# First layer of a two-layer cross-attention kernel: weighted sum issued behind the scores, three transposed groups finished in their own slot

## The chip, the cores and the metric

The kernel runs on one core of one Trainium2 chip. The time is the device time of one execution in microseconds (us). Three runs of the kernel before took 1789.04, 1791.48 and 1791.99, median 1791.48. A core has five engines with a queue of instructions each: TensorE (PE), VectorE (DVE), ScalarE (ACT), GpSimd (POOL) and SyncE (SP, which here only issues DMAs). They meet only in semaphores.

## What is computed

The input x is 8 batches of 56 rows by 256; the context is 8 batches of 1500 rows by 256. The first layer, the only one the change touches, cut to what matters:

```python
a = _layer_norm(audio_kv, ln_gamma, ln_beta)          # context, 8 x 1500 x 256
Q, K, V = hidden_states @ Wq.T, a @ Wk.T, a @ Wv.T    # 16 heads of 16 columns
scores = einsum('bhtd,bhsd->bhts', Q, K) * scale + mask
attn = softmax(scores, axis=-1)
out = einsum('bhts,bhsd->bhtd', attn, V) @ Wo.T
x = hidden_states + tanh(gate) * out
```

Two cross-attentions with 16 heads of 128 columns and an MLP follow. All matrix products are made of high and low parts: a value is split into a part that TensorE's fast format holds (high) and the rest (low), and three products high·high, high·low, low·high are summed.

## The kernel before

**Slots.** The first layer is 64 slots: 8 batches (`b`) of 8 head pairs (`t`, 0 to 7), `g = 8b + t`. A slot has 112 rows (two heads of 56 queries) and 1500 context columns. Each engine has a function `slot(b, t, n, kind)` which says what it issues in a slot, and `whole_batches` calls it for all slots: batches 0 to 5 are of kind "full", 6 of kind "keys", 7 of kind "plain"; batches 1 to 4 run in a hardware loop. The order within `slot` is written out by hand, and there is no scheduler.

**The path of one slot g.**
- TensorE makes the scores: 3 matmuls of 500 columns into PSUM banks 0 to 2 (`scores`, L841). They wait until the exponential of slot g−1 has read the banks.
- VectorE takes the negated row maximum over all three banks (`row_max`, L1742, written to `neg0`).
- ScalarE makes the exponential with that bias into `prob0` (`softmax`, L1299), with the row sums beside it.
- TensorE turns the 12 chunks of 128 columns of `prob0` in three groups of 4 (`transposes`, L853). Group 0 goes to PSUM bank 3, group 1 to bank 4, group 2 to bank 3 again. Groups 0 and 1 wait for the low parts of the slot before, group 2 for the low part of group 0 of its own slot.
- ScalarE copies a turned group as high part into `pt0` (`high_probs`, L1247, tile pt), and VectorE subtracts it for the low part (`low_probs`, L1667, tile pt).
- TensorE makes the weighted sum: 12 matmuls on `pt0` and the values `v3`, into bank 7 (`weighted`, L870). It waits for all six parts of its slot.
- ScalarE copies the second half of it to `ost` (`output`, L1305), and VectorE adds the first half (`collapse`, L1763, tile o_c).

**Beside it, for the batches to come.** In slots 0 to 5 of kinds "full" and "keys" TensorE makes one sixth of the next batch's keys (`keys`, 6 matmuls of 500 columns into bank 5, L770 to L772), ScalarE copies it to `kst` (L1247), GpSimd splits it into `khl` (L604, L579), and SyncE stacks the parts into `k3` (L393 to L396, 5 DMAs for a head pair). In slots 0 to 3, 6 and 7 TensorE makes one sixth of the values (`values`, 12 matmuls of 256 columns into bank 6), which ScalarE copies at the head of its next slot and VectorE splits there (tile v). For the batch after the next, kind "full" only, VectorE takes statistics of the raw context in slots 0, 1 and 2 (`load_stats`, L1674 and L1680, 4 chunks each), GpSimd makes the factors (`variance`, L583 and L585), TensorE turns them (`turn_stats`, L780), ScalarE sends them to memory and back as one long row for all partitions (`spread_stats`), GpSimd scales the context by it (`scale`, L590) and splits it with ScalarE (`ct_low`, `ct_high`). In slot 4 TensorE spreads the reciprocals of the batch before over the partitions (`spread`, L877).

**How a slot is staged before the change.** In slot g TensorE issues: scores of g+1, group 2 of g−1, keys, weighted sum of g−1, groups 0 and 1 of g, values. ScalarE: high part of group 2 of g−1, copy of the values, copy of the keys, exponential of g+1, copy of the weighted sum of g−1, high parts of groups 0 and 1 of g. VectorE: maximum of g+1, low part of group 2 of g−1, low part of the values, statistics (slots 1 and 2), collapse of g−1, low parts of groups 0 and 1 of g, statistics (slot 0).

**The start.** Before the slots the same engines make the queries, the centred weights (`w0`), the statistics and the split of the contexts of batches 0 and 1, the keys of batch 0 in six groups (`K_FIRST`) and its values. GpSimd's queue there is: factors of batch 0, low parts of the weights, scale of the last third of context 0 (L674), factors of batch 1, low part of that third, three key groups, two scales of batch 1. VectorE's `load_stats(1, k)` stands between the centred weights and the splits of the queries (L1707).

## Time and profile before

| what | value |
|---|---|
| median of 3 runs | 1791.48 us |
| profiled execution | 1799.13 us, span 1797.3 us |
| mean granted TensorE clock | 0.973 |
| TensorE busy | 1672.9 us (93%) |
| VectorE busy | 1203.6 us (67%) |
| ScalarE busy | 1041.9 us (58%) |
| GpSimd busy | 902.7 us (50%) |
| from 0 to 460 us: TensorE busy | 376.49 us |
| from 460 us on: TensorE busy | 1296.36 of 1337.30 us |

The span runs from the first to the last instruction of the profiled execution; its own time is 1.8 us longer. Busy time counts instructions at work. The first 460 us are the first layer. The granted clock is 1.00 for 2.4 GHz and 0.5 for 1.2 GHz; a stretch between has had both.

### The profile page before, as it was taken

The page shows a single profiled execution, that of the slowest core. Times are in us where ns is not written, and L with a number is a line of the kernel's source. Part 1 is how long each engine was busy: PE and PEld are TensorE (multiplying, and loading weights), DVE is VectorE, ACT ScalarE, POOL GpSimd, SP SyncE. Part 2 cuts the span into 40 slices and gives each one's busy share as a digit, 9 for nine tenths or more (in the row PEclk, how much of TensorE's full clock was granted, in tenths as well). Part 3 has the DMA queues.
Part 4 walks back from the last instruction along what each step waited for, and adds up shares of the span by engine and source line. Part 5 has one row for each costly group of instructions (what it writes and reads, how often), then busy time and mean ns, then how long its engine had stood idle before and what let it go on. Part 6 is the DMA issues. An engine that isn't in the chain of part 4 may idle for free.

```text
span 1797.3 us, 36860 instructions
## 1 busy us (share of the span) xinstructions
PE 1672.9 (93%) x12520; PEld 1576.3 (88%) x12520; DVE 1203.6 (67%) x2340; ACT 1041.9 (58%) x2023; POOL 902.7 (50%) x655
## 2 busy tenths in 40 slices
PE   4788988997899999999999999999999999999997
PEld 3677877786789999999999987889999999999986
DVE  5577777777356766766766766466676677677673
ACT  2467766676264655656656555545665656556563
POOL 4456665542144545536535547453653554455483
PEclk8899999999699999999999999899999999999998
DMA  7967666746221111111211114221121121120031
GB/s 211 234 161 183 180 173 177 179 115 167 73 81 62 54 50 37 64 41 36 70 35 36 70 32 131 62 85 37 36 70 36 35 70 36 36 70 1 2 91 40
DMA packets 109995, 150.81 MB, mean 84 GB/s; under 512 B 25540, under 2 KB 95684, under 8 KB 109828
## 3 DMA queue, kind: packets, MB, share of 16 engines
q1 hardware_dynamic: 108484, 142.45, 28.4%
q10 hardware_dynamic: 1344, 6.19, 1.0%
q8 instruction: 98, 1.61, 0.4%
q14 instruction: 69, 0.57, 0.1%
HBM read 108.32 MB, written 3.42 MB: 62 GB/s over the span
## 4 chain that ended last, share of the span: by engine, by line
PE 67%; DVE 10%; ACT 3%; issue 2%; SPq 1%; POOL 1%; DMA 1%; ACTq 0%; DVEq 0%; POOLq 0%
PE ps L770 12%; PE ps L772 11%; PE ps L771 11%; PE ps L1025 7%; PE ps L1029 7%; PE ps L1027 7%; PE ps L960 2%; DVE ar L1866 2%; PE ps L1005 2%; PE ps L992 1%; DVE neg L1742 1%; PE ps L853 1%; PE ps L870 1%; DVE ar L1911 1%; ACT prob L1299 1%
## 5 line engine op out<-in xcount | busy, mean ns | idle before, releaser
L722 POOL TENSOR_TENSOR rr<-ar,rr 125x512 fp32r<-125x512 f32 x336 | 455.3, 1387 | 406.6 <-ACT rr L1483 398.7
L1025 PE MATMUL ps<-cx,rr 125*128 125x258 f32 x1344 | 396.6, 295 | 0.0
L1029 PE MATMUL ps<-cx,rr 125*128 125x258 f32 x1344 | 379.6, 282 | 0.0
L1027 PE MATMUL ps<-cx,rr 125*128 125x256 f32 x1344 | 379.3, 282 | 0.0
L770 PE MATMUL ps<-rr,ct 128*125 128x256 f32 x1152 | 329.6, 286 | 4.5 <-DVE ar L1911 2.7
L772 PE MATMUL ps<-rr,ct 128*125 128x256 f32 x1152 | 324.7, 282 | 0.0
L771 PE MATMUL ps<-rr,ct 128*125 128x256 f32 x1152 | 324.7, 282 | 0.0
L1470 ACT ACTIVATE ar<-ar 125x512 f32<-125x512 f32 x336 | 208.5, 626 | 84.5 <-DVE ar L1911 59.4
L1027 PEld LDWEIGHTS ps<-cx,rr 125*128 125x128 f32 x1344 | 254.9, 190 | 0.0
L1029 PEld LDWEIGHTS ps<-cx,rr 125*128 125x128 f32 x1344 | 254.8, 190 | 0.0
L1025 PEld LDWEIGHTS ps<-cx,rr 125*128 125x128 f32 x1344 | 253.6, 189 | 0.1
L770 PEld LDWEIGHTS ps<-rr,ct 128*125 128x125 f32 x1152 | 215.2, 187 | 7.7 <-issue 5.8
L772 PEld LDWEIGHTS ps<-rr,ct 128*125 128x125 f32 x1152 | 215.6, 187 | 0.0
L771 PEld LDWEIGHTS ps<-rr,ct 128*125 128x125 f32 x1152 | 215.3, 187 | 0.0
L1483 ACT ACTIVATE rr<-ar 125x512 fp32r<-125x512 f32 x336 | 202.1, 621 | 0.0
L1850 DVE TENSOR_TENSOR ar<-ps,ar 125x512 f32<-125x512 f32 x186 | 128.5, 691 | 92.3 <-PE ps L772 86.9
L1911 DVE TENSOR_TENSOR ar<-ps,ar 125x512 f32<-125x512 f32 x288 | 182.9, 682 | 4.9
L1462 ACT ACTIVATE extra<-lbq,negm 128x1 f32<-128x1 f32 x112 | 27.7, 286 | 215.9 <-DVE negm L1894 215.9
L579 POOL TENSOR_TENSOR w_s<-w_raw,w_s 128x512 fp32r<-128x512 f32 x72 | 95.0, 1320 | 110.3 <-ACT w_s L1247 103.6
L1247 ACT ACTIVATE pt<-ps 128x448 fp32r<-128x448 f32 x192 | 96.5, 536 | 71.4 <-PE ps L853 71.0
L870 PE MATMUL ps<-pt,v 128*66 128x224 f32 (+1 forms) x768 | 101.8, 273 | 37.2 <-DVE pt L1667 37.2
L870 PEld LDWEIGHTS ps<-pt,v 128*66 128x66 f32 (+1 forms) x768 | 82.9, 138 | 52.3 <-issue 45.5
(210 smaller groups left out, 3778.6 us busy)
## 6 DMA issues: line engine op xcount, KB each, us to landing
raw_t<-in_ctx_t SPq DMA_DIRECT2D x24, 1500.0 KB, 6.7
k<-khl SPq DMA_DIRECT2D x192, 187.5 KB
raw<-in_ctx SPq DMA_DIRECT2D x16, 1500.0 KB
raw<-in_ctx SPq DMA_DIRECT2D x8, 1408.0 KB
raw<-stat_scratch ACTq DMA_DIRECT2D x7, 750.0 KB, 3.9
w_raw<-in_wq SPq DMA_DIRECT2D x32, 128.0 KB, 2.3
w_raw<-in_wk SPq DMA_DIRECT2D x32, 128.0 KB, 2.2
qo<-in_wqt SPq DMA_DIRECT2D x32, 128.0 KB, 3.2
```

The source lines that it names most:

```text
L722: pool.tensor_tensor(group(p[:, 1, :, :], u, k), x, f(group(p[:, 0, :, :], u, k)), ALU.subtract)\
L770: eng.matmul(out, w_hi, x_hi, start=start, stop=False, skip_group_check=True)
L771: eng.matmul(out, w_hi, x_lo, start=False, stop=False, skip_group_check=True)
L772: return eng.matmul(out, w_lo, x_hi, start=False, stop=stop, skip_group_check=True)
L870: mm = pe.matmul(ps[0:2 * PW + 2, 7, 0:2 * QR], v3[n][0:m, v:v + 2 * PW + 2], pt0[0:m, c, :], start=c == 0, stop=c == CH - 1)
L1025: pe.matmul(ps[:, bank, 0:D + 2], hi, cx[0:KC, c, 0:D + 2], start=c == 0, stop=False, skip_group_check=True)
L1027: pe.matmul(ps[:, bank, 0:D], hi, cx[0:KC, c, D + 2:CW], start=False, stop=False, skip_group_check=True)
L1029: mm = pe.matmul(ps[:, bank, 0:D + 2], lo, cx[0:KC, c, 0:D + 2], start=False, stop=c == CH - 1, skip_group_check=True)
L1470: act.activation(group(xp, u, k), group(xp, u, k), ACT.Exp).then_inc(s["exp_done"], 1)
L1483: act.activation(group(p_buf[u][:, 0, :, :], u, k), group(xp, u, k), ACT.Copy).then_inc(s["p_hi"], 1)
L1850: dve.tensor_tensor(run[0:KC, :], src, run[0:KC, :], ALU.max).then_inc(s["run_step"], 1)
L1911: dve.tensor_tensor(x, src, m, ALU.add).then_inc(s["s_free"], 1)
```

## The change

In the first layer the third group of transposes moves out of the next slot and into its own, on all three engines, and the exponential moves up on ScalarE. In slot g TensorE now issues: scores of g+1, weighted sum of g−1, groups 0 and 1 of g, keys, group 2 of g, values. ScalarE: copy of the values, exponential of g+1, copy of the weighted sum of g−1, high parts of groups 0, 1 and 2 of g, copy of the keys. VectorE: maximum of g+1, low part of the values, collapse of g−1, low parts of groups 0 and 1 of g, statistics (slots 0 to 2), low part of group 2 of g. The turned statistics go through bank 7 instead of bank 5. GpSimd's second scale comes before the keys of slot 5 instead of after them. At the start `load_stats(1, k)` moves on VectorE behind the splits of context 0, the second context is loaded after all constants, and the statistics of batch 1 are turned after the fourth key group instead of the second and sent for after the sixth instead of the fourth. No operation is added or taken away.

```diff
@@ SyncE
                     n_const += 1
-                    if n_const == 10:
-                        sp.wait_ge(s["bn_done"], 3)
-                        load_raw(0, 1)
...
             constants()
+            sp.wait_ge(s["bn_done"], 3)
+            load_raw(0, 1)
@@ GpSimd, slot
+                if kind == "full" and t == 5:
+                    scale(b + 2, 1)
                 if t in K_AT and kind != "plain":
...
                 if kind == "full":
-                    if t in (4, 5):
-                        scale(b + 2, t - 4)
+                    if t == 4:
+                        scale(b + 2, 0)
@@ TensorE, slot
                     scores(b if t < SLOTS - 1 else b + 1, (t + 1) % SLOTS, g + 1)
                 if t or later:
-                    transposes(g - 1, (t - 1) % SLOTS, 2)
-                if t in K_AT and kind != "plain":
-                    u = K_N[t]
-                    pe.wait_ge(s["zks"], 6 * (b + 1) + u)
                     if t == 4 and kind == "full":
                         pe.wait_ge(s["stat_row"], b + 3)
-                    keys(b + 1, u, *K_AT[t], 5)
-                if t or later:
                     weighted(b if t else b - 1, (t - 1) % SLOTS, g - 1, n if t else 1 - n)
                 transposes(g, t, 0)
                 transposes(g, t, 1)
+                if t in K_AT and kind != "plain":
+                    u = K_N[t]
+                    pe.wait_ge(s["zks"], 6 * (b + 1) + u)
+                    keys(b + 1, u, *K_AT[t], 5)
+                transposes(g, t, 2)
                 if t == 3 and kind == "full":
-                    pe.wait_ge(s["zks"], 6 * (b + 1) + 4)
-                    turn_stats(b + 2, 5)
+                    pe.wait_ge(s["zoc"], g)
+                    turn_stats(b + 2)
@@ ScalarE, slot
-                if t or later:
-                    high_probs(g - 1, 2)
...
-                if t in K_AT and kind != "plain":
-                    u = K_N[t]
-                    act.wait_ge(s["zkl"], 6 * (b + 1) + u - 4)
-                    keys(b + 1, u, 5)
...
                 high_probs(g, 0)
                 high_probs(g, 1)
+                high_probs(g, 2)
+                if kind == "full" and t == 3:
+                    turn_stats(b + 2)
+                if t in K_AT and kind != "plain":
+                    u = K_N[t]
+                    act.wait_ge(s["zkl"], 6 * (b + 1) + u - 4)
+                    keys(b + 1, u, 5)
@@ VectorE, start
-            for k in range(3):
-                load_stats(1, k)
             for jc in range(DH):
...
                 low(ct[:, 1, :, v], raw_t[:, :, v], ct[:, 0, :, v]).then_inc(s["zcv"], 1)
+            for k in range(3):
+                load_stats(1, k)
@@ VectorE, slot
                     row_max((t + 1) % SLOTS, g + 1)
-                if t or later:
-                    low_probs(g - 1, 2)
...
                     values(b + 1 if t else b, u_last, 1 - n if t else n, 6)
+                if t or later:
+                    collapse(b if t else b - 1, (t - 1) % SLOTS, g - 1)
+                low_probs(g, 0)
+                low_probs(g, 1)
                 if t == 0 and later:
                     reciprocals(b - 1, 1 - n)
-                if kind == "full" and t in (1, 2):
+                if kind == "full" and t < 3:
                     load_stats(b + 2, t)
...
-                if t or later:
-                    collapse(b if t else b - 1, (t - 1) % SLOTS, g - 1)
-                low_probs(g, 0)
-                low_probs(g, 1)
-                if kind == "full" and t == 0:
-                    load_stats(b + 2, 0)
+                low_probs(g, 2)
```

The first place is TensorE, slot 6 of the first batch. `ps<-k,q` are the scores, `ps<-ident,prob` the transposes (x4 is one group), `ps<-pt,v_0` the weighted sum, `ps<-wv_s,ct` the values. Before:

```order
L841 MATMUL ps<-k,q 112x500 x3
L853 MATMUL ps<-ident,prob 128x112 x4
L870 MATMUL ps<-pt,v_0 66x224 x12
L853 MATMUL ps<-ident,prob 128x112 x8
L770 MATMUL ps<-wv_s,ct 128x256
```

After:

```order
L842 MATMUL ps<-k,q 112x500 x3
L871 MATMUL ps<-pt,v_0 66x224 x12
L854 MATMUL ps<-ident,prob 128x112 x12
L771 MATMUL ps<-wv_s,ct 128x256
L772 MATMUL ps<-wv_s,ct 128x256
```

The four transposes of group 2 stood behind the next scores and are now the last of twelve, ahead of the values.

The second place is VectorE, slot 2 of the first batch. `neg` is the maximum, `pt` a low part of a group, `v_1` that of the values, `o_c` the collapse. Before:

```order
L1742 TENSOR_REDUCE neg<-ps 112x1
L1667 TENSOR_TENSOR pt<-ps,pt 128x4x112
L1667 TENSOR_TENSOR v_1<-ps,v_1 128x32x16
L1674 BN_STATS bn<-raw 128x6 x4
L1680 BN_AGGR mv<-bn 128x2 x4
L1763 TENSOR_TENSOR o_c<-ps,ost 32x56 x2
L1667 TENSOR_TENSOR pt<-ps,pt 128x4x112 x2
```

After:

```order
L1737 TENSOR_REDUCE neg<-ps 112x1
L1662 TENSOR_TENSOR v_1<-ps,v_1 128x32x16
L1758 TENSOR_TENSOR o_c<-ps,ost 32x56 x2
L1662 TENSOR_TENSOR pt<-ps,pt 128x4x112 x2
L1669 BN_STATS bn<-raw 128x6 x4
L1675 BN_AGGR mv<-bn 128x2 x4
L1662 TENSOR_TENSOR pt<-ps,pt 128x4x112
```

The low part of group 2 went from behind the maximum to the end of the slot before it, and the statistics from ahead of the collapse to ahead of that low part.

The third place is VectorE at the start: `v_1` are the query splits, `raw_t` and `ct` the scale and split of context 0. Before:

```order
L1674 BN_STATS bn<-raw 128x6 x4
L1680 BN_AGGR mv<-bn 128x2 x4
L1707 SCALAR_TENSOR_TENSOR v_1<-ps,par_s,v_1 128x448 x4
L1711 TENSOR_SCALAR ra<-rbc 96x125
L1713 COPY bias<-ps 128x4
L1718 TENSOR_TENSOR raw_t<-raw_t,o_c 128x2x500 x2
L1667 TENSOR_TENSOR ct<-raw_t,ct 128x2x500 x2
```

After:

```order
L1706 COPY bias<-ps 128x4
L1711 TENSOR_TENSOR raw_t<-raw_t,o_c 128x2x500 x2
L1662 TENSOR_TENSOR ct<-raw_t,ct 128x2x500 x2
L1669 BN_STATS bn<-raw 128x6 x4
L1675 BN_AGGR mv<-bn 128x2 x4
L1723 CAST khl<-kst 128x500
```

The statistics of batch 1 (three such pairs of rows) moved from ahead of the query splits to behind the context splits, ahead of the first key split.

## Rows read from the trace of the kernel before

**Rows 1.** Windows of the first layer, cut at maxima: span, busy us (x instructions), clock

```profile
core 0: us, PE busy (x) PEld busy (x) DVE busy (x) ACT busy (x) POOL busy (x), PEclk, DMA share, GB/s
76.35:119.16 42.81, 37.01 (x268) 32.33 (x267) 32.70 (x66) 28.24 (x54) 23.10 (x16) 0.96 0.61 155
119.16:366.36 247.20, 222.11 (x1648) 193.84 (x1647) 194.26 (x396) 171.89 (x326) 144.19 (x105) 1.00 0.73 180
366.36:414.70 48.34, 45.27 (x331) 40.43 (x330) 34.19 (x56) 31.77 (x62) 15.05 (x15) 0.96 0.51 120
414.70:446.69 31.99, 23.02 (x171) 19.25 (x169) 23.37 (x39) 24.07 (x43) 10.30 (x5) 0.95 0.63 157
```

**Rows 2.** Windows of two slots, cut at maxima: slot 1 of batch 6, slot 6

```profile
372.28:378.22 5.94, 5.94 (x48) 5.42 (x47) 4.42 (x7) 4.11 (x8) 1.27 (x2) 1.00 0.79 179
304.45:310.39 5.94, 4.59 (x41) 4.20 (x40) 3.82 (x8) 4.68 (x8) 4.21 (x3) 1.00 0.35 77
```

**Rows 3.** Timeline, a slot of the last batch: start, us, engine, line, tiles [idle before]

```profile
431.04 1.72 DVE L1742 TENSOR_REDUCE neg<-ps 112x1 f32<-112x1500 f32 x1
...
432.86 1.51 ACT L1299 ACTIVATE prob<-ps,neg 112x1500 f32<-112x1500 f32 x1 [0.77 <-DVE neg L1742]
...
434.36 0.24 ACT L1305 ACTIVATE ost<-ps 64x112 f32<-64x112 f32 x1
...
434.70 0.43 DVE L1763 TENSOR_TENSOR o_c<-ps,ost 32x56 f32<-32x56 f32 x2 [1.41 <-ACT ost L1305]
...
435.16 1.16 DVE L1667 TENSOR_TENSOR pt<-ps,pt 128x448 fp32r<-128x448 f32 x2
...
435.84 0.60 PE L853 MATMUL ps<-ident,prob 112*128 112x112 f32 x4 [0.33 <-DVE pt L1667]
...
436.24 1.71 DVE L1742 TENSOR_REDUCE neg<-ps 112x1 f32<-112x1500 f32 x1
```

**Rows 4.** Timeline, slots 1 and 2 of batch 6, with keys and values

```profile
375.82 0.36 PE L770 MATMUL ps<-wv_s,ct 128*128 128x256 f32 x1
...
377.33 0.85 PE L841 MATMUL ps<-k,q 97*112 97x500 f32 x3
...
378.02 0.55 PE L853 MATMUL ps<-ident,prob 112*128 112x112 f32 x4
...
378.22 1.72 DVE L1742 TENSOR_REDUCE neg<-ps 112x1 f32<-112x1500 f32 x1 [0.17 <-PE ps L841]
...
378.34 0.47 PE L770 MATMUL ps<-ct,wk_s 128*128 128x500 f32 x1
...
378.61 0.55 ACT L1247 ACTIVATE pt<-ps 128x448 fp32r<-128x448 f32 x1 [1.42 <-PE ps L853]
```

**Rows 5.** Chain that ended last, in order of time: start, us, what

```profile
393.85 0.77 PE ps L877 x4
...
455.39 0.55 ACT pt L1247
455.96 0.64 DVE pt L1667
```

**Rows 6.** Timeline of ScalarE, VectorE and GpSimd at the start

```profile
25.68 2.19 ACT L1274 ACTIVATE v<-ps,par_s 128x448 fp32r<-128x448 f32 x4
...
29.21 2.43 DVE L1707 SCALAR_TENSOR_TENSOR v<-ps,par_s,v 128x448 fp32r<-128x448 f32 x4
...
34.04 2.31 DVE L1667 TENSOR_TENSOR ct<-raw_t,ct 128x1000 fp32r<-128x1000 f32 x2
...
74.56 1.41 DVE L1674 BATCH_NORM_STATS2 bn<-raw 128x6 f32<-128x256 f32 x4 [1.05 <-DMA raw<-in_ctx]
...
30.86 2.31 POOL L585 TENSOR_TENSOR mv<-mv,mhalf 128x12 f32<-128x12 f32 x1
...
36.13 2.45 POOL L579 TENSOR_TENSOR ct<-raw_t,ct 128x1000 fp32r<-128x1000 f32 x1 [2.96 <-ACT ct L1247]
...
55.25 6.68 POOL L590 TENSOR_TENSOR raw_t<-raw_t,raw 128x1500 f32<-128x1500 f32 x2 [8.40 <-DMA raw_t<-in_ctx_t]
```

**Rows 7.** Window of slot 6 of batch 6, with a dip of the clock

```profile
401.26:408.77 7.51, 6.16 (x41) 5.77 (x40) 3.92 (x8) 3.38 (x6) 0.26 (x1) 0.77 0.90 193
```

More of the change, by code:

```diff
@@ L886, in slot @@
                 if t or later:
-                    transposes(g - 1, (t - 1) % SLOTS, 2)
+                    if t == 4 and kind == "full":
+                        pe.wait_ge(s["stat_row"], b + 3)
+                    weighted(b if t else b - 1, (t - 1) % SLOTS, g - 1, n if t else 1 - n)
+                transposes(g, t, 0)
+                transposes(g, t, 1)
                 if t in K_AT and kind != "plain":
@@ L920, in _ @@
                 keys(0, n, *K_FIRST[n], (5, 3)[n % 2])
-                if n == 1:
+                if n == 3:
                     pe.wait_ge(s["stat_row"], 1)
@@ L934, in _ @@
             whole_batches(pe, slot, "full", "keys", "plain")
-            transposes(GT0 - 1, SLOTS - 1, 2)
             weighted(B - 1, SLOTS - 1, GT0 - 1, 1)
@@ L1790, in slot @@
                 low_probs(g, 1)
-                if kind == "full" and t == 0:
-                    load_stats(b + 2, 0)
+                if t == 0 and later:
+                    reciprocals(b - 1, 1 - n)
+                if kind == "full" and t < 3:
+                    load_stats(b + 2, t)
+                if kind == "plain" and t == SLOTS - 1:
+                    reciprocals(b, n)
+                low_probs(g, 2)
             for n in range(6):
```

27 lines of the change are left out of this document (6 added, 21 removed).

## The prediction

> **What bounds the kernel now.** I read the windows of the first layer first, cut at VectorE's maxima (L1742), since each of them opens a slot. Eight slots make a batch. From 119.16 to 366.36 five batches take 247.20 us, 49.44 each; the batch that still makes keys and values but no statistics takes 48.34; six slots of the last batch take 31.99, so 5.33 each [rows 1]. The second view is single slots [rows 2]: slot 1 of the batch without statistics takes 5.94 and slot 6 of an earlier one the same. Everything behind the first layer is untouched by the change.
>
> Then the timeline, where the reader is to see two things that are nearly equally long. One is TensorE's own work: in a slot with keys and values it is busy for all of the 5.94 us [rows 2]. The other is a ring through VectorE and ScalarE, uncovered in the last batch [rows 3]: call the start of a maximum R. The exponential starts at R+1.82, the weighted sum is copied out at R+3.32, VectorE folds it at R+3.66, its low part of group 0 starts at R+4.12, that of group 1 follows, and the next maximum starts at R+5.20. TensorE's third transposes start at R+4.80, released by the low part of group 0. They wait there because groups 0 and 2 share a PSUM bank. Today nothing on the ring stands behind them: the scores went out before them, and their split comes in the next slot, after the next maximum.
>
> **The change, part by part.** *The third group in its own slot.* TensorE now issues the third transposes ahead of the values and of the next scores. ScalarE has put the exponential ahead of all splits, so the low part of group 0, which releases them, still can't start before R+4.12. What was beside the ring is now on it. The links, from rows:
> - Low part of group 0 to third transposes 0.68 [rows 3], so they start at R+4.80.
> - Transposes to the next TensorE group 0.32, to ScalarE's split 0.59; twelve value matmuls 1.51; scores to maximum 0.89 [rows 4].
> - ScalarE's split to VectorE's low part 0.57; the spread matmuls, where slot 4 has them, 0.77 [rows 5].
> - One low part 0.54, half of the two in 435.16 to 436.24 [rows 3].
>
> There are two ways to the next maximum, and the later one counts.
> - Through TensorE, with values (slots 0 to 3, 6, 7): 4.80+0.32+1.51+0.89 = 7.52. Slot 4, spread in place of values: 4.80+0.32+0.77+0.89 = 6.78.
> - Through VectorE: 4.80+0.59+0.57+0.54 = 6.50. This one decides in slot 5 and in the last batch.
>
> *Statistics.* One round of four bn_stats and four bn_aggr is 1.79, from its start at 74.56 [rows 6] to the maximum at 76.35 with which the first window opens [rows 1]. In slots 1 and 2 it lay in VectorE's wait for the copied sum; it now stands between the low parts of groups 1 and 2: 5.20+1.79+0.54 = 7.53, the same as TensorE's way, so it costs nothing more. In slot 0 the reciprocal is there too, about 7.65. Slot 3 has the turned statistics, which I put at 7.55.
>
> A batch with statistics is then 7.65+2×7.52+7.55+6.78+6.50+2×7.52 = 58.6 against 49.44. For five: +45.6. The batch without statistics, 6×7.52+6.78+6.50 = 58.4 against 48.34: +10.1. Six slots of the last batch, 6×6.50 = 39.0 against 31.99: +7.0. Seven slots of the first batch took 42.81 [rows 1] and get 50.9: +8.1.
>
> *Key copies on ScalarE move behind the splits.* They held the exponential up by about 0.5 us in key slots, but TensorE hid that; now the new ring replaces it. Gain in the sum: none. GpSimd gets its key group some 4 us later in a slot. Its keys feed SyncE's stacking, and the first stack of the next batch is wanted only when slot 7 begins. That is 15 us behind, since the slots are longer too. I take nothing; a late stack is in the range. GpSimd's second scale moves ahead of the keys of slot 5: nobody waits for these before the fifth stack.
>
> *The start.* The second batch's statistics leave VectorE's queue ahead of the query splits and go behind the context splits. The query splits, four in 2.43 from 29.21, wait for ScalarE's four (25.68 to 27.87, the first pair at about 26.8), so they can start some 2.3 us earlier, and with them the context splits, which then end at 34.1 instead of 36.4 (34.04+2.31) [rows 6]. There the three rounds of 1.79 begin, and they end at 39.5. But GpSimd's queue is unchanged: its two statistics steps (2.31 and a short one before it, some 2.6) stand ahead of the split of the last context third, which started at 36.13 and now can't before 39.5+2.6 = 42.1. TensorE's third key group waits for it, and VectorE's key splits stand behind the same rounds. The statistics row is turned two key groups later and sent after all six. The two scales of the second batch began at 55.25, on a context transfer [rows 6]; this transfer is issued once the late split is done, at about 42.1+2.45 = 44.6, but the statistics row, sent some 9 us later than today, comes back at about 62 by my estimate. They then start 6 or 7 us later, and with them the third context load, whose landing ended VectorE's wait at 74.56 [rows 6]. In the changed order that wait also holds the third group. Bounds: nothing, if the transfers land no later than today, and 9, if all of it adds up. I take +6.5 at the third maximum. Loading the context after the constants costs nothing itself: it is issued about 5 us later and wanted at 34.
>
> *The end.* The last third group no longer has a step of its own; I take −1.
>
> *TensorE's clock.* Between 119.16 and 366.36 the granted clock is 1.00 [rows 1]. In the last two batches it dips to 1.2 GHz now and then, at the price of 7.51 for a slot 6 [rows 7] that takes 5.94 at full clock [rows 2]. With longer idle stretches I expect one short dip per batch more, about 0.6 each: +4. Bounds: 0, and 1.57 in each of slots 5 to 7 of seven batches, 33.
>
> **Sum.** 6.5+8.1+45.6+10.1+7.0−1+4 = 80.3. The profiled execution took 1799.13 (span 1797.3) and would take 1879.4; the median of the runs is 7.65 lower, so 1791.48+80.3 = 1871.8. I give 1872.
>
> **Rivals.** *The clock falls in the lightly loaded slots.* Slots 6 and 7 go from 77% busy, 4.59 of 5.94 [rows 2], to 4.6 of 7.5, near 61%. Against it: the last batch is 72% busy by its row (23.02 of 31.99) and still got 0.95 [rows 1]. With 33 in place of 4 it gives 1901. The Trainium skill (TensorE: Matmul & The Clock Gate, "A second HAM failure mode: psum-queue depth-cycling") tells of a kernel whose matmul groups idle briefly between PSUM banks, and whose clock swings between its two levels for it; by that rule this rival would be the forecast, with its 1901. The trace of before, with short gaps in every batch and no dip in 247 us, speaks against it.
>
> *The ring never reaches TensorE (not slower).* The place is the third transposes of a full slot. Of its 5.94 us of work TensorE has all but the transposes' 0.32 and the values' 1.51 ahead of them, 4.1, and its scores start 0.89 before R. So there is no wait if the low part of group 0 ends by R+3.2. Then a full slot stays at 5.94, a batch with statistics can at most shed the 1.1 by which it is longer than the one without (49.44 against 48.34), 6.6 over six, and if the start gains its 2.3 on the query splits instead of losing, the time is 1791.5−8.9 = 1782.6. The ring puts that end at R+4.73 [rows 3], 1.5 too late, and the exponential cannot be passed on ScalarE. Only links of the ring shorter than in all slots that I read would help.
>
> *The stack comes late.* If the keys of slot 4 reach SyncE so late that slot 7 waits 2 us in each of six batches for its first stack, it is 12 more, 1884.
>
> *The change doesn't do what it says.* The exponential is ahead of the splits in the order, but in time it was already: in the last batch nothing but the maximum holds it [rows 3]. So that half brings nothing there, in any of the cases.
>
> **How the numbers follow.** Forecast 0.80; clock 0.10; stack 0.05; not slower 0.05. The forecast's own bounds: a link wrong by 0.2 us in some 55 slots is 11, the start 6.5 down and 2.5 up, the clock's 4 down. That gives 1850 to 1886; with the late stack and most of the clock rival the range is 1846 to 1896. Within 0.2% (3.6 us, what a measurement of this kernel can tell from no change) there is hardly a case: 0.02; faster 0.03; slower 0.95.
>
> **What would show it.** In the profile after: maxima 7.5 us apart in slots with values and 6.5 in the last batch; third transposes with a wait of about 1.4 us for VectorE's low part; VectorE idle between the low parts of groups 1 and 2 where no statistics stand; the third key group at the start delayed by about 5 us; the same times behind the first layer. Wrong would be: slots of 6 us, no wait ahead of the third transposes, or a clock well below 0.9 from 120 us on.

## The result, and the profile after

| | kernel before | changed kernel |
|---|---|---|
| median of the runs, one chip | 1790.74 us | 1895.56 us |
| lowest and highest | 1789.04 and 1791.99 | 1890.76 and 1899.89 |
| profiled execution | 1799.13, span 1797.3 | 1890.76, span 1888.9 |
| mean granted TensorE clock | 0.973 | 0.962 |

The changed kernel takes 1.0578 times as long as the kernel before, 95% interval 1.0555 to 1.0600. That is 104.8 us slower. The forecast was 1872 with a range of 1846 to 1896: the direction and the mechanism came out, and the time lies 0.4 us inside the top of the range.

The windows of the changed kernel, cut at maxima at the same places as [rows 1]: rest of the first batch, batches 1 to 5, batch 6, last batch.

```profile
core 0: us, PE busy (x) PEld busy (x) DVE busy (x) ACT busy (x) POOL busy (x), PEclk, DMA share, GB/s
79.23:131.44 52.21, 41.39 (x274) 35.99 (x275) 33.34 (x64) 29.30 (x55) 23.11 (x16) 0.90 0.61 151
131.44:438.71 307.27, 231.02 (x1647) 202.17 (x1646) 197.91 (x395) 173.62 (x326) 144.32 (x105) 0.96 0.58 143
438.71:501.10 62.39, 48.16 (x331) 42.47 (x329) 34.94 (x56) 32.80 (x63) 15.07 (x15) 0.92 0.37 90
501.10:542.86 41.76, 28.52 (x168) 25.14 (x167) 23.83 (x39) 23.31 (x42) 10.32 (x5) 0.77 0.48 127
```

TensorE's work in batches 1 to 5 is hardly more than before, 231.02 against 222.11, and the stretch is 60.1 longer. So TensorE now waits. The list of waits from 80 to 560 us says for whom (total us, times, longest):

```profile
engine line waited for: us in total, times, longest us
...
PE ps L854 <- DVE pt L1662: 117.3, 63, 3.3
ACT prob L1297 <- DVE neg L1737: 116.7, 62, 5.2
DVE o_c L1758 <- ACT ost L1303: 104.9, 64, 4.1
...
DVE neg L1737 <- PE ps L842: 37.2, 31, 2.6
```

In 63 slots TensorE stands ahead of a group of transposes until VectorE's low part is done, 117.3 us in all. VectorE waits for the weighted sum's copy and ScalarE for the maximum. Each waits for the next: this is a ring. One turn of it, in slots 1 and 2 of batch 6 (the place of [rows 4]), by the timeline:

```profile
start us, us, engine line op out<-in xcount [idle before <-releaser]
...
453.85 1.72 DVE L1737 TENSOR_REDUCE neg<-ps 112x1 f32<-112x1500 f32 x1 [0.91 <-PE ps L842]
...
455.66 1.51 ACT L1297 ACTIVATE prob<-ps,neg 112x1500 f32<-112x1500 f32 x1 [1.90 <-DVE neg L1737]
...
457.16 0.24 ACT L1303 ACTIVATE ost<-ps 64x112 f32<-64x112 f32 x1
457.31 0.95 ACT L1245 ACTIVATE pt<-ps 128x448 fp32r<-128x448 f32 x2
457.51 0.43 DVE L1758 TENSOR_TENSOR o_c<-ps,ost 32x56 f32<-32x56 f32 x2 [1.34 <-ACT ost L1303]
457.97 1.16 DVE L1662 TENSOR_TENSOR pt<-ps,pt 128x448 fp32r<-128x448 f32 x2
...
458.65 0.60 PE L854 MATMUL ps<-ident,prob 112*128 112x112 f32 x4 [1.46 <-DVE pt L1662]
...
459.03 0.37 PE L771 MATMUL ps<-wv_s,ct 128*128 128x256 f32 x1
...
460.54 0.85 PE L842 MATMUL ps<-k,q 97*112 97x500 f32 x3
...
461.43 1.72 DVE L1737 TENSOR_REDUCE neg<-ps 112x1 f32<-112x1500 f32 x1 [0.93 <-PE ps L842]
```

Maximum, exponential, copy of the sum, collapse, low part of group 0, third transposes, values, scores, next maximum: 461.43−453.85 = 7.58. In the kernel before this slot took 5.94 [rows 2]. The links stand at +1.81, +3.31, +3.66 and +4.80 after the maximum; the prediction had +1.82, +3.32, +3.66 and +4.80.

The difference of the two profiled executions, in us:

| stretch | before | after | difference | forecast |
|---|---|---|---|---|
| start to the third maximum | 76.35 | 79.23 | +2.9 | +6.5 |
| rest of the first batch | 42.81 | 52.21 | +9.4 | +8.1 |
| batches 1 to 5 | 247.20 | 307.27 | +60.1 | +45.6 |
| batch 6 | 48.34 | 62.39 | +14.1 | +10.1 |
| last batch up to its last maximum | 31.99 | 41.76 | +9.8 | +7.0 |
| from there to the last copy `ost` | 12.57 | 15.59 | +3.0 | −1 |
| clock, a term of its own | | in the rows above | | +4 |
| rest of the program and its end | 1339.87 | 1332.31 | −7.6 | 0 |
| sum | 1799.13 | 1890.76 | +91.6 | +80.3 |

The −7.6 lies where nothing was changed. In size it answers to the 7.65 by which the profiled execution before was above its median. The first layer is then 99.2 us longer in these two executions, and the medians differ by 104.8; where the other 5.6 lie isn't known.

### The profile page after: what moved, and what is told of

It reads as the page before. It is cut to its first block, busy times and chain, and to the rows that moved or that the text cites. A ratio compares the mean times of both kernels' runs of the same rounds, so it can differ in the third digit from the quotient of the medians.

```text
span 1888.9 us, 36878 instructions
## 1 busy us (share of the span) xinstructions
PE 1687.4 (89%) x12520; PEld 1589.0 (84%) x12520; DVE 1209.5 (64%) x2340; ACT 1044.2 (55%) x2023; POOL 904.3 (48%) x655
## 4 chain that ended last, share of the span: by engine, by line
PE 61%; DVE 12%; issue 5%; ACT 4%; POOL 1%; ACTq 0%; DVEq 0%; POOLq 0%
PE ps L771 11%; PE ps L773 10%; PE ps L772 10%; PE ps L1023 7%; PE ps L1027 7%; PE ps L1025 7%; DVE neg L1737 3%; ACT prob L1297 2%; DVE ar L1857 2%; PE ps L958 2%; PE ps L1003 1%; DVE pt L1662 1%; PE ps L990 1%; DVE ar L1902 1%; PE ps L854 1%
## 5 line engine op out<-in xcount | busy, mean ns | idle before, releaser
L854 PE MATMUL ps<-ident,prob 112*128 112x112 f32 x768 | 104.3, 275 | 117.8 <-DVE pt L1662 117.8
L854 PEld LDWEIGHTS ps<-ident,prob 112*128 112x128 f32 x768 | 83.3, 148 | 141.0 <-DVE pt L1662 140.7
L1297 ACT ACTIVATE prob<-ps,neg 112x1500 f32<-112x1500 f32 x64 | 96.9, 1513 | 121.0 <-DVE neg L1737 121.0
```

The source lines that it names most:

```text
L854: mm = pe.transpose(ps[:, 3 + k % 2, (c % GRP) * QR:(c % GRP) * QR + QR], prob0[0:QR, t % 2, c * P:(c + 1) * P], ident[0:QR, 0:QR])
L1297: act.activation(prob0[0:QR, t % 2, 0:S].rearrange("p (j t) -> p j t", j=3), ps[0:QR, 0:3, 0:SB], ACT.Exp, bias=neg0[:, t % 2:t % 2 + 1], ...
```

## The experiments

Twelve kernels were run. Each row gives the median, and the ratio to the kernel before on the same chip with its interval. On these chips the kernel before itself had medians from 1789.6 to 1793.5, so a difference of 3 us between two rows is not clear of noise.

| kernel | median us | ratio | interval |
|---|---|---|---|
| changed slots, old start | 1892.33 | 1.0557 | 1.0516 to 1.0597 |
| third group behind the values | 1859.38 | 1.0369 | 1.0331 to 1.0407 |
| split of group 0 first, both engines | 1801.14 | 1.0040 | 1.0021 to 1.0060 |
| the same, ScalarE alone | 1940.84 | 1.0844 | 1.0822 to 1.0866 |
| filler in slots 6 and 7 | 1881.61 | 1.0486 | 1.0446 to 1.0527 |
| own bank for some third groups | 1856.90 | 1.0360 | 1.0339 to 1.0381 |
| before, key copy late | 1794.62 | 1.0021 | 1.0000 to 1.0042 |
| combined slots, old start | 1781.66 | 0.9950 | 0.9931 to 0.9968 |
| combined slots, new start | 1790.47 | 0.9990 | 0.9978 to 1.0002 |
| before, new start | 1796.75 | 1.0025 | 1.0004 to 1.0046 |
| before, new start, GpSimd mended | 1792.17 | 1.0003 | 0.9985 to 1.0020 |
| combined, new start, GpSimd mended | 1782.13 | 0.9948 | 0.9930 to 0.9966 |

### 1. Slots or start?

The changed kernel with the start of the kernel before (its diff undone at SP, TensorE, ScalarE and VectorE's `load_stats(1, k)`).

> The changed kernel with the start of the kernel before (second context loaded among the constants, its statistics on VectorE ahead of the query splits, its statistics row turned after the second key group). Theory: the start costs what the profile after shows at the third maximum, 79.23 against 76.35 us, so this run is some 3 us faster than the changed kernel's 1895.6: about 1893. Rival, the 6.5 us of the prediction: about 1889. In both the slots stay at 7.56 to 7.7 with values and 6.56 in the last batch.

It took 1892.33, 3 less than the changed kernel, but the intervals of the two ratios overlap (1.0516 to 1.0597 and 1.0555 to 1.0600). So the slots are the cause of nearly all of the 104.8 us, and this run can't tell the start's share from nothing or from the 6.5 of the rival; section 8 comes back to it. The waits of TensorE for VectorE's low part were the same, 121.3 us in 62 slots.

### 2. Is the third group's place on TensorE in the ring?

```diff
@@ TensorE, slot, of the changed kernel
-                transposes(g, t, 2)
...
                 if kind == "plain" and t == SLOTS - 1:
                     pe.wait_ge(s["zks"], 6 * B)
                     spread(b, 5)
+                transposes(g, t, 2)
```

> The changed kernel, but TensorE issues the third transposes behind the values and the spread, as the last thing of the slot. Ring theory: TensorE's way to the next maximum becomes 4.80+0.32+0.89 = 6.0 and VectorE's way of 6.56 decides. Slots 3, 6 and 7 fall from about 7.6 to 6.56, slot 4 from 7.0 to 6.56, slots 0 to 2 stay at 7.56 for the statistics; the batch without statistics has all slots at 6.56. That is 3.7 per batch times 6, plus 6.3, plus some of the clock dips of slots 6 and 7, about 5: 1895.6-33 = about 1862. Rival (the slots are long for VectorE or ScalarE alone, whatever stands behind the third transposes): no change, 1895.

It took 1859.38, 36 less than the changed kernel. One turn in batch 6:

```profile
423.47 1.71 DVE L1737 TENSOR_REDUCE neg<-ps 112x1 f32<-112x1500 f32 x1
...
428.26 0.60 PE L854 MATMUL ps<-ident,prob 112*128 112x112 f32 x4 [0.38 <-DVE pt L1662]
428.63 0.91 PE L842 MATMUL ps<-k,q 97*112 97x500 f32 x3
...
430.01 1.71 DVE L1737 TENSOR_REDUCE neg<-ps 112x1 f32<-112x1500 f32 x1
```

The third transposes start at +4.79 after the maximum, as before; only the values now lie ahead of them, and the slot is 6.54. So the way around is fixed as far as these transposes. What TensorE puts between them and the next scores is added to every slot. In batches 1 to 5 slots 0 to 2 stayed at 7.48 to 7.70, as expected: there VectorE's statistics (1.79) stand between low parts 1 and 2, the 7.53 of the prediction's VectorE way. Slot 3, expected at 6.56, stayed at 7.63 to 7.85 and has no statistics. Its trace in batch 2 shows another wait: TensorE's turned statistics stand ahead of the values there and wait 1.35 for VectorE's collapse, so that the third transposes start 6.01 after the maximum instead of 4.79.

### 3. The order of exponential and split

```diff
@@ ScalarE, slot, of the changed kernel
+                high_probs(g, 0)
                 if not (kind == "plain" and t == SLOTS - 1):
...
                 if t or later:
                     output(g - 1)
-                high_probs(g, 0)
@@ VectorE, slot
+                low_probs(g, 0)
                 if t or later:
                     collapse(b if t else b - 1, (t - 1) % SLOTS, g - 1)
-                low_probs(g, 0)
```

> The changed kernel, but ScalarE copies the high part of group 0 ahead of the exponential, and VectorE takes its low part ahead of the collapse. Ring theory: the exponential is no longer ahead of what releases the third transposes, their wait goes, full slots fall to TensorE's 5.94, those with statistics to VectorE's sum of about 6.2, the last batch to about 5.5: some 48.5 per batch against 49.4 before the change, 2.4 more in the last batch, 2.9 more at the start: 1787 to 1795. Rival (a third group in its own slot costs its three steps in a row wherever the exponential stands): 1860 or more.

It took 1801.14, 94 of the 105 back; the theory's upper end was 1795. In the last batch:

```profile
433.97 1.71 DVE L1737 TENSOR_REDUCE neg<-ps 112x1 f32<-112x1500 f32 x1
...
435.22 0.54 ACT L1245 ACTIVATE pt<-ps 128x448 fp32r<-128x448 f32 x1 [1.10 <-PE ps L854]
435.77 1.51 ACT L1297 ACTIVATE prob<-ps,neg 112x1500 f32<-112x1500 f32 x1
435.80 0.62 DVE L1662 TENSOR_TENSOR pt<-ps,pt 128x448 fp32r<-128x448 f32 x1
...
436.48 0.60 PE L854 MATMUL ps<-ident,prob 112*128 112x112 f32 x4 [0.91 <-DVE pt L1662]
...
439.15 1.71 DVE L1737 TENSOR_REDUCE neg<-ps 112x1 f32<-112x1500 f32 x1
```

The third transposes start at +2.51 instead of +4.79, while the exponential runs, and the slot is 5.18. The exponential itself is hardly moved, +1.80 against +1.81: ScalarE was idle until the maximum was done, and the high part fits into that gap. What the expectation missed are the statistics: in batch 2 slots 1 and 2 take 7.07 and slot 3 takes 6.93. In slots 1 and 2 VectorE now waits 0.92 for the copy `ost` with the statistics still behind it.

Does ScalarE's half alone do it? The same edit without VectorE's part:

> Changed kernel with only ScalarE's high part of group 0 back ahead of the exponential; VectorE's collapse stays ahead of its low part. Ring theory: VectorE's low part of group 0 still waits behind the collapse, and the collapse for the copy of the weighted sum behind the exponential, so nothing of the 95 us that the two moves together gave back is gained; and the exponential now also waits for group 0's transposes, which end 1.8 to 2.3 us after the maximum starts, plus the 0.55 of the high part, so it starts at 2.4 to 2.85 instead of 1.82: 0.6 to 1.0 more a slot, 1930 to 1955 in all. Rival: ScalarE's order is what matters (the low part follows the high part at once, the collapse is short): most of the gain of the two moves together, 1800 to 1820.

It took 1940.84, 45 more than the changed kernel. Slot 0 of batch 6:

```profile
484.29 1.72 DVE L1737 TENSOR_REDUCE neg<-ps 112x1 f32<-112x1500 f32 x1 [0.93 <-PE ps L842]
...
485.92 0.55 ACT L1245 ACTIVATE pt<-ps 128x448 fp32r<-128x448 f32 x1 [1.66 <-PE ps L854]
...
486.36 1.51 ACT L1297 ACTIVATE prob<-ps,neg 112x1500 f32<-112x1500 f32 x1
...
488.19 0.43 DVE L1758 TENSOR_TENSOR o_c<-ps,ost 32x56 f32<-32x56 f32 x2 [1.59 <-ACT ost L1303]
```

The high part of group 0 is ready at 486.47 and is of no use yet: VectorE's queue has the collapse first, which waits 1.59 for the copy behind the exponential. Nothing of the 94 us is gained: VectorE's order alone is enough to close the ring. The other half, VectorE's order changed and ScalarE's not, wasn't run. By the lines of the changed kernel it would gain next to nothing: ScalarE's high parts begin at 457.31 behind the exponential, and one takes 0.54, so the first is there at about 457.85, and VectorE's low part starts at 457.97 already. Each of the two queues holds the ring by itself.

The total was as expected, but not its make-up. The exponential starts at +2.07, 0.26 later and not 0.6 to 1.0, since group 0's transposes end sooner than I had read. Slots 0 to 3 of batch 6 take 7.80 to 7.83, 0.25 more than in the changed kernel. Over 60 slots that is some 15 us, so by this estimate the larger part of the 45 is the clock: in batch 2 (205.16 to 274.53) the granted clock is 0.87 and the batch takes 69.37, where the changed kernel had 0.97 and 61.29. Slots of 8 and 9 us are common there.

### 4. The clock in the light slots

The changed kernel dips once in each of batches 0 to 5, in slot 6 or 7, and in both slots of batch 6; two more dips lie in slot 4 of batch 5 and in the last batch. Slots 6 and 7 of batch 2, by windows (columns as above), and TensorE at the fall, by the timeline:

```profile
237.40:245.08 7.68, 4.38 (x38) 3.91 (x37) 3.92 (x8) 4.89 (x9) 4.69 (x5) 1.00 0.90 229
245.08:254.11 9.03, 6.10 (x41) 5.48 (x40) 4.49 (x7) 5.05 (x10) 4.08 (x3) 0.82 1.06 235
```

```profile
249.97 0.60 PE L854 MATMUL ps<-ident,prob 112*128 112x112 f32 x4 [2.93 <-DVE pt L1662]
...
250.66 0.28 PE L773 MATMUL ps<-wv_s,ct 128*128 128x256 f32 x1
250.77 0.34 PE L771 MATMUL ps<-wv_s,ct 128*128 128x256 f32 x1
250.91 0.41 PE L772 MATMUL ps<-wv_s,ct 128*128 128x256 f32 x1
...
252.62 1.45 PE L842 MATMUL ps<-k,q 97*112 97x500 f32 x3
```

After a slot in which TensorE worked 4.38 of 7.68, and a wait of 2.93, its matmuls go from 0.28 to 0.41 each (0.12 and 0.21 apart) and the scores from 0.85 to 1.45, all on the ring. To test it, eight matmuls whose product nobody reads were added in these slots, in the wait:

```diff
@@ TensorE, slot, of the changed kernel
+            def filler(b, t, kind):
+                if t in K_AT or kind == "plain":
+                    return
+                pe.wait_ge(s["zks"], 6 * (b + 2))
+                for n in range(8):
+                    pe.matmul(ps[:, 5, :], wk_s[:, 0, 0, 0:P], wk_s[:, 1, :, :].rearrange("p h d -> p (h d)"),
+                              start=True, stop=True)
...
+                filler(b, t, kind)
                 transposes(g, t, 2)
```

> The changed kernel with eight matmuls of 512 columns on constants, into the idle bank 5, ahead of the third transposes in slots 6 and 7 of batches 0 to 6, where TensorE waits about 3 us. They compute nothing that is used. Clock theory: the dips to 1.2 GHz in slots 6 and 7 come from TensorE's idling there and are gone, slots 6 and 7 all at 7.7: about 12 us faster than the changed kernel, 1884, and less spread between runs; the last batch, without them, keeps its dips. Rival (the dips come whatever these slots hold): the same 1895 or a little more.

It took 1881.61, 14 less although it computes more. The windows of the same two slots:

```profile
236.43:244.08 7.65, 6.20 (x45) 5.27 (x44) 3.91 (x8) 4.86 (x9) 4.68 (x5) 1.00 0.86 219
244.08:251.75 7.67, 6.58 (x49) 5.71 (x48) 4.51 (x7) 4.53 (x9) 4.14 (x2) 1.00 1.07 235
```

TensorE is busy 6.20 and 6.58 of the slots, the clock stays at 1.00, and slots 6 and 7 of all seven batches lie between 7.55 and 7.87. The filler stands in a wait that is there anyway. Added up, these fourteen slots take 107.1 us instead of 119.0. So the clock in slots 6 and 7 is 12 of the 105, as was expected; the other 2 of the 14 lie where no filler stands.

### 5. The shared PSUM bank

Group 2 waits for the low part of group 0 because both use bank 3. Bank 5, the keys', is free in slots 6 and 7 and in the last batch, so there group 2 went into it.

```diff
@@ planner, of the changed kernel
+        def third_bank(t, kind):
+            return 5 if (t < SLOTS - 1 if kind == "plain" else t not in K_AT) else 3
@@ TensorE, transposes
-                if k == 2:
+                if k == 2 and bank == 3:
                     pe.wait_ge(s["zpl"], 3 * g + 1)
@@ TensorE, slot
+                if third_bank(t, kind) == 5:
+                    pe.wait_ge(s["zks"], 6 * B if kind == "plain" else 6 * (b + 2))
-                transposes(g, t, 2)
+                transposes(g, t, 2, third_bank(t, kind))
```

> The changed kernel, but in slots 6 and 7 of batches 0 to 6 and slots 0 to 6 of the last batch the third group is turned into the idle bank 5 and so need not wait for the low part of group 0. If sharing a bank is what puts TensorE's third transposes on the ring, only VectorE's three low parts in a row are left of it there: R+4.12 and 1.62 more, 5.75. Slots 6 and 7, 119.0 us in all seven batches after the change, become 14 times 5.75 to 5.95, the last batch 7 times 0.8 less, and the dips of slots 6 and 7 go: 1895.6-36-7 = about 1852. Rival (they wait for something else, such as ScalarE's queue): no change, 1895.

It took 1856.90, 39 less. Slots 6 and 7 of batches 0 to 5 fell to 5.71 to 5.83 and the last batch's to 5.71 to 5.80: without the bank's wait the ring no longer passes TensorE's third transposes. Slots 1 to 5 stayed nearly as they were. In batch 6 slots 6 and 7 took 8.50 and 6.52, because the scores of slot 6 waited 3.46 for a stacking transfer of the last batch (`q<-q_scratch`), which the longer slots of the changed kernel had hidden. Some of the gain went to the clock, which fell in another place. The windows of slot 6 of batch 2 and slot 0 of batch 3:

```profile
230.51:236.34 5.83, 5.19 (x42) 4.31 (x41) 3.73 (x7) 4.18 (x9) 4.13 (x4) 1.00 0.81 194
...
242.16:251.45 9.29, 7.36 (x43) 6.45 (x42) 6.15 (x17) 4.64 (x9) 4.18 (x3) 0.82 0.99 229
```

Slot 0, where the wait for the shared bank begins again (1.93 ahead of the third transposes), took 8.80, 9.29, 9.29, 9.20 and 8.59 at the head of batches 1 and 3 to 6 (7.76 in batch 2). Why the fall comes there and not in slot 1 stays open.

### 6. One part alone on the kernel before

```diff
@@ ScalarE, slot, of the kernel before
-                if t in K_AT and kind != "plain":
+                if t == 3 and kind == "full":
                     u = K_N[t]
...
                 high_probs(g, 1)
+                if t in K_AT and kind != "plain" and not (t == 3 and kind == "full"):
+                    u = K_N[t]
+                    act.wait_ge(s["zkl"], 6 * (b + 1) + u - 4)
+                    keys(b + 1, u, 5)
```

> The kernel before, with one part of the change alone: ScalarE copies the keys behind its split of group 1, so that the exponential starts as soon as its maximum is there (slot 3 of batches 0 to 5 keeps its copy, since the turned statistics share the bank). Theory: TensorE's own 5.94 us hid the copy in slots 0 to 2, so nothing changes there; slots 4 and 5 may shed up to 0.5 each. Between no change and 6 us faster than the kernel before. Rival (a key copy that comes later holds TensorE's next keys or GpSimd): slower by 3 us or more.

It took 1794.62, a ratio of 1.0021 with one end of the interval at no change, where no change to 6 us faster was expected. Slots 4 and 5 fell as expected, to 5.30 and 5.29, from 5.9 and 5.6. But slot 3 took 7.29, 10.75 and 9.12 in batches 1, 4 and 5, and slot 6 took 7.4 in two batches. In slot 3 of batch 4 GpSimd's key split comes late:

```profile
285.25 0.60 POOL L604 CAST khl<-kst 128x500 fp32r<-128x500 f32 x1 [10.33 <-DMA q<-q_scratch]
```

GpSimd waits 10.33 for a stacking transfer, ScalarE's key copy waits 3.11 for GpSimd, and in this slot the copy still stands ahead of the exponential, which starts only 4.88 after the maximum. The same wait makes slot 3 late in kernels without this edit: 6.86 in batch 5 of the kernel before and 9.68 in batch 4 of the start alone (section 8). So it can't be put down to the move alone. Why the transfer is late in some batches and not in others stays open, and the move is no gain as measured.

### 7. A version that beats both

Experiment 3 named the two places left: statistics ahead of the collapse, as in the kernel before, where VectorE idles for `ost` anyway, and the turned statistics last.

```diff
@@ VectorE, slot, of the kernel of experiment 3
                 low_probs(g, 0)
-                if t or later:
-                    collapse(b if t else b - 1, (t - 1) % SLOTS, g - 1)
-                low_probs(g, 1)
                 if t == 0 and later:
                     reciprocals(b - 1, 1 - n)
                 if kind == "full" and t < 3:
                     load_stats(b + 2, t)
+                if t or later:
+                    collapse(b if t else b - 1, (t - 1) % SLOTS, g - 1)
+                low_probs(g, 1)
@@ ScalarE, slot: turn_stats(b + 2) of slot 3 moved behind the key copy
@@ TensorE, slot: turn_stats(b + 2) of slot 3 moved behind the values
```

> The kernel of the run with group 0 split ahead of the exponential, with three more edits: the statistics stand on VectorE behind the low part of group 0 and ahead of the collapse, where it waits for ScalarE; the turned statistics are TensorE's last work of slot 3; the start is that of the kernel before. Theory: slots 0 to 2 fall from 7.07 to VectorE's own sum of about 6.25, slot 3 from 6.94 to 5.94, the others stay at 5.3 to 5.65: 46.5 per batch against 50.2 there and 49.4 before the change. 1801.1-23-3 = about 1775, faster than the kernel before by 1%. Rival (VectorE has no room for the statistics there and they push the collapse and the next maximum): 1795 or more.

> The same with the start of the change. Theory: slower by the 3 us that the start cost in the run with the slots alone, about 1778. Rival (the start costs nothing, or the 6.5 of the prediction): the same, or 1781.5.

With the start of the kernel before it took 1781.66, 0.9950 of it (0.9931 to 0.9968): the only set of slots that beats both kernels, the kernel before by 9 us. About 1775 was expected. In batch 1 slot 0 took 7.23 where 6.25 was expected. All slots of that batch were 7.23, 6.08, 6.21, 5.76, 5.54, 5.28, 5.30 and 5.66. Slots 4 to 7 are shorter than those of the kernel before, at 5.9, 5.6, 5.9 and 5.9, and slot 0 still waits for a context transfer (0.79 in batch 2). The late key copy alone gives slots 4 and 5 their 5.3 (section 6); slots 6 and 7 fell to some 5.3 and 5.65 only here and in experiment 3. So the third group in its own slot seems to be worth something, provided nothing that waits for the exponential stands ahead of the split of group 0, but no run has it by itself. Slot 6 of batch 6 took 8.41, with 2.22 of waiting for the stacking transfer again: the late stack that the prediction had as a rival shows once the slots are short. With the change's start the same slots took 1790.47, which gives the whole gain back. These 9 us needed their own test.

### 8. What the start costs

The change's start on the kernel before, then the same with GpSimd's factors behind the split that TensorE waits for, and then that start under the combined slots:

```diff
@@ GpSimd, start, in the last two
-            variance(1)
             ct_low(0, 2)
+            variance(1)
```

> Kernel before with the change's start alone (statistics of batch 1 behind the context splits on VectorE, the second context loaded after the constants, the turning after the fourth key group), its slots untouched. Theory A: the start costs what the maxima of the changed kernel showed, 3 us (79.23 against 76.35 at the third maximum), so about 3 over the kernel before. Theory B: in the changed slots part of the delay was hidden, since the third maximum there comes in a longer ring anyway; with short slots the start costs the 6.5 that the two fast versions of slots showed at their third maximum (82.11 against 75.59) and some more after it, 7 to 9 over the kernel before.

> As the run before, and at the start GpSimd's factors of batch 1 (2.3 us and a short step) stand behind the low part of the last third of context 0 instead of ahead of it. If what the start costs is that this low part, and TensorE's third key group behind it, wait for VectorE's late statistics (GpSimd waited 8.86 us there in the changed kernel), the third key group comes some 6 us earlier than in the run before and the time falls to within 2 us of the kernel before, or below it. If instead the late statistics row and the scales behind it set the end (the transfer at whose landing VectorE's wait ended), the time stays within 2 us of the run before.

> The combined version of the slots with the change's start, and GpSimd's factors behind the late split as in the run before. With the old start these slots took 1781.66, with the change's start 1790.47. If the order of GpSimd's queue is what the start costs, it is back at 1780 to 1784; if the late statistics row is, it stays at 1788 to 1791.

The start alone gave 1796.75, a ratio of 1.0025 (1.0004 to 1.0046), so 1 to 8 us slower, which doesn't decide between the two theories. With GpSimd mended it was 1792.17, no difference from the kernel before. Under the combined slots the mending brought 8 back, 1790.47 to 1782.13. GpSimd in the changed kernel:

```profile
28.73 3.31 POOL L675 TENSOR_TENSOR raw_t<-raw_t,o_c 128x1000 f32<-128x1000 f32 x1 [2.48 <-DMA o_c<-stat_scratch]
40.91 0.25 POOL L582 TENSOR_SCALAR mv<-mv 128x12 f32<-128x12 f32 x1 [8.86 <-DVE mv L1675]
41.23 2.69 POOL L584 TENSOR_TENSOR mv<-mv,mhalf 128x12 f32<-128x12 f32 x1
43.89 2.28 POOL L578 TENSOR_TENSOR ct<-raw_t,ct 128x1000 fp32r<-128x1000 f32 x1
```

and TensorE's third key group behind it:

```profile
46.32 0.76 PE L771 MATMUL ps<-ct,wk_s 128*128 128x500 f32 x1 [6.79 <-POOL ct L578]
...
49.65 0.38 PE L773 MATMUL ps<-ct,wk_s 128*128 128x500 f32 x1
```

GpSimd stood 8.86 us for VectorE's late statistics with the split behind them in its queue. TensorE stood 6.79 for the split, and came out of it at the lower clock: its key matmuls took 0.62 instead of 0.38 until 49.4. In the mended kernel the split stands first and starts at 35.32:

```profile
35.32 2.45 POOL L578 TENSOR_TENSOR ct<-raw_t,ct 128x1000 fp32r<-128x1000 f32 x1 [3.13 <-ACT ct L1246]
41.05 0.25 POOL L582 TENSOR_SCALAR mv<-mv 128x12 f32<-128x12 f32 x1 [3.28 <-DVE mv L1678]
```

The mended order brings two things forward at once and so doesn't separate them: the third key group, which TensorE now takes without a wait, and the statistics row, which is turned behind it and is sent for at 50.88 instead of 55.64 under the combined slots.

The third maximum came at 82.11 with the change's start and 75.59 with the old one under the combined slots, and at 79.23 and 76.35 in the kernels that the prediction compared. Theory B, that long slots hide part of the start, isn't borne out by the traces: the changed kernel with filler, whose first slots are just as long, had it at 80.95, and the start alone, with short slots, at 80.69. All eight kernels with the change's start as it is lie between 79.23 and 82.11, and the four with the old one between 74.76 and 76.35.

## Why the prediction was right, and what it had wrong

**The ring.** Right in each link, within 0.06 us, and in what ties it: the slots with values took 7.56 (7.52 forecast), those of the last batch 6.55 (6.50), the third transposes waited 1.46 (about 1.4). Experiments 2, 3 and 5 cut the ring at three places. Each shortened the slots that it was aimed at by about what was expected, but for slot 3 in experiment 2 and the slots with statistics in experiment 3.

**The exponential's place.** "In time it was ahead already" was right, and half of the story. Experiment 3 shows it starting at the same point with the high part in front. The harm is what stands behind it: the high part of group 0 on ScalarE, and the low part behind the collapse on VectorE. The kernel with ScalarE's order alone mended, 1940.84, shows that VectorE's is enough to keep the ring; by the lines of the changed kernel ScalarE's is too, which no run tested.

**The clock, the term that was mis-sized.** The step was "one short dip per batch more, about 0.6 each: +4". There was one dip in each of six batches, in slot 6 or 7, as forecast, but each cost 1.2 to 2.1. Batch 6 had both slots long (9.68 and 8.99), slot 4 of batch 5 took 7.64 instead of 6.88, and the last batch had 8.62 and 6.92 instead of 6.55. Over their plain lengths these slots add up to some 15. The kernel before had 2.3 of its own (7.51 [rows 7] against 5.94, and one of 5.96 against 5.20), and the forecast lengths of the slots after left these out, so the +4 stood for the whole 15 and is 11 short. The rival of 33 us was too dear, since after a dip the clock was back within a slot or two. I had priced a dip by its being short, and not by what lies under it: the values and the scores run at 1.2 GHz on the ring itself. The row for it was there, the 1.57 of [rows 7] against [rows 2]. The last batch shows the other side. From 507.66 to 527.32, at a granted clock of 0.76, three slots took 6.55 to 6.56, no more than at full clock: there the slow stretch fell on the weighted sum (2.07 in place of 1.40 at 513.89) and on the first eight transposes (1.58 in place of 0.93 at 515.75), which the ring leaves out, while the third transposes and the scores ran at full clock (0.61 at 519.01 and 0.91 at 519.38). The Trainium skill (TensorE: Matmul & The Clock Gate, "A second HAM failure mode: psum-queue depth-cycling") tells of a clock that swings where matmul groups idle between banks. This case's trace agrees that the clock falls where TensorE idles, 0.82 in the 9.03 us slot, but what came before was one wait of 2.93 us; the brief gaps of the kernel before went with 1.00 for 247 us [rows 1]. The price in slots 6 and 7, where the filler stood, was 12 us.

**Slots in the hardware loop.** I read every link outside the loop [rows 3, 4]. In batches 1 to 4 a slot takes 7.68 instead of 7.56, since the collapse starts 0.45 after the copy begins (273.40 and 272.95) instead of 0.35 (457.51 and 457.16). The kernel before has the same two gaps. There they lie beside TensorE's own work. In the changed kernel it makes 4 us. What in the loop makes the gap longer isn't shown.

**The end, −1, which was +3.0.** The step "the last third group no longer has a step of its own" seems to have left out a step that is moved: the last reciprocals went on VectorE from ahead of the collapse to behind the low parts. GpSimd takes them at 553.49, TensorE's spread waits 1.15 for GpSimd, and the last weighted sum, queued behind the spread, starts at 555.84 and runs at the lower clock (2.56; the window from 542.86 to 558.45 has 0.73). This is read from the trace; no run separates it.

**The start, +6.5, which was +2.9 in this kernel.** The chain was right: GpSimd's split at 43.89 (42.1 or later), TensorE's third key group at 46.32 instead of 39.66 (about 5 later). The term that was mis-sized is the return of the statistics row. It was sent for 10.4 us later (53.69 against 43.31, 9 forecast), and the scales began at 59.35 (about 62), which is 4.1 later and not 6 to 7. This return differs between executions with the same start: the scales began 5.7 us after the row was sent for here and 8.7 after it in the kernel with filler, where the third maximum came at 80.95. So the 2.9 is in part luck of this execution; under the combined slots the two starts were the forecast 6.5 apart.

**The late stack and "not slower"** didn't come in this kernel: no slot 7 without a dip was longer than its neighbours, and no full slot was under 6.5. In the experiments with short slots the late stack did come, once, in slot 6 of batch 6: in experiments 3, 5, 6 and 7 the next batch's first scores waited 2.0 to 3.5 for it.

**The sum.** 80.3 was forecast and 99.2 measured up to the end of the layer: the clock 11 short, the loop 4, the end 4, the start 3.6 too much. The remaining 3 or 4 are small change, above all in slots 3 and 4 of batches 1 to 5, which took 7.77 to 7.86 and, without a dip, 6.99 to 7.03, where 7.55 and 6.78 were forecast. Slot 4 of the first batch was priced with a spread that it doesn't have, 6.78, and took 6.57. The time of 1895.56 is beyond the forecast's own upper bound of 1886. It is inside the range only by what two rivals had added to it: the late stack, which didn't come, and the clock, which was there for the right reason and at the wrong price. That it fell inside by 0.4 us is luck; the forecast of the ring is not.

## What to carry to other kernels

In a hand-ordered pipeline draw the ring of who waits for whom over one period, and put nothing that waits for the ring's long step (here the collapse, for the exponential) ahead of a short one that others wait for, on any queue. A group that shares a buffer with another in the same slot brings that buffer's whole read-back into the ring; it is harmless only if the read-back comes before the long step. And price a clock dip by the instructions that run on the critical path at half clock, not by its length.

## What the runs showed of the hardware

At the start VectorE's two scales of the context took 2.30 in the kernel before, [rows 6], beginning at 31.75, and 4.42 in the changed kernel, beginning at 28.69; GpSimd's took 2.29 and 3.31 (28.73, the row above). In the changed kernel they run at the same time, in the other one after the other. Alone the two are 4.59 together, and side by side both were done 4.42 after the first began, so they nearly took turns. By the Trainium skill (SBUF — State Buffer, "SBUF: two separate sides") VectorE and GpSimd have one pair of ports in common, which is held for a whole instruction; the trace agrees. Because of this, more than half of the query splits' gain at the start, which the prediction counted as 2.3, was lost: the scales began 3.1 earlier than in the kernel before, and the context splits behind them only 1.0 earlier (33.03 against 34.04). They ended at 35.4 instead of the 34.1 forecast.

A filler of eight matmuls in a wait, whose product nobody reads, made the kernel 14 us faster; 12 of it are slots that kept the full clock.

A granted clock of 0.76 cost nothing in three slots of the last batch, 6.55 us each as at full clock, where the slow stretch fell on matmuls beside the ring.
